# Odd chunks' feed-forward redistributed over the next batch's stages: 4, 4, 24 and 16 steps

## The chip, the cores and the metric

One core of one Trainium2 chip. The metric is the device time of one launch in microseconds (us). The engines are named as in the profile: PE is TensorE (PEld its weight loads), DVE is VectorE, ACT is ScalarE, POOL is GpSimd, SP is SyncE, which here issues all DMAs.

## The reference, cut to what matters

Two transformer layers on x (4 batches, 1024 tokens, 512 features) with a context of 64 tokens per batch. Cut to its shape:

```python
# layer 0: attention of x to the context, 16 heads, biased, then a layer norm
x = ln(softmax(q(x) @ k(ctx).T / 8 + 2 * fside) @ v(ctx) @ wo + bo + x)
# layer 1
x = attn(ln1(x), ln1(x)) + x        # self-attention, 16 heads of 32, 8-bit rounding of q, k, v, weights
x = attn(ln2(x), ctx) + x           # context attention, the same rounding
a, g = split(ln3(x) @ ff_w1 + ff_b1)   # 512 -> 2 x 2048
x = a * gelu(g) @ ff_w2 + ff_b2 + x    # 2048 -> 512
```

All unrounded products are made of three matmuls (high by high, high by low, low by high part), written by `three` (L1720).

## The kernel before, in words

A batch is two chunks of 512 tokens (CH), so there are eight chunks n = 0 to 7. For each batch the program runs four kinds of stage: `cross(n)` for both chunks (context attention of layer 0, the layer norms, and the projections q1, k1, v1), then for each chunk `self_attention(n)` and `middle(n)` (output projection, layer norm, second context attention, layer norm). I call them the A, S and M stages of a chunk. The feed-forward of a chunk has no stage of its own. Its 48 steps (F_STEPS, L45: four each of g0 a0 g1 d0 a1 g2 d1 a2 g3 d2 a3 d3) are hosted by later stages: each step is 12 matmuls of 128x512, in four quarters of three, into PSUM bank 6 or 7 in turn. A "g" step is taken out of PSUM by ACT (L1226), and the fourth is followed by a Gelu over all four (L1232); an "a" step is multiplied in by DVE (L1514), then split by ACT (L1218) and POOL (L1008); a "d" step is added to x by DVE (L1477). A step's bank must be emptied before the second step after it can begin (`wait_empty` in `feed`, L1899).

Every engine walks the same list of slots, and each slot of a stage may host quarters; `host_quarters` (L72) makes the list, `feed` on each engine takes from it what falls to that engine. Each engine executes strictly in this written order. A has 18 slots: slot 0, slots 1 to 11 beside the softmax steps, slots 12 to 15 before the transposes of the four 128-token tiles (`norm_T`, L1976 to L1978), called the tail here, and two more that PE fills with nothing. S has 71 slots, one per unit of 128 queries and one head. M has 23: 0 to 5 output projection, 6 to 9 projection q2, 10 to 18 the second context attention, 19 to 22 the last transposes.

Even chunks (FROM_S, L88) are hosted by the S and M stages of the next chunk, 28 and 20 steps. Odd chunks 1, 3 and 5 (`begins_in_A`, L93; FROM_A, L89) are hosted by both A stages, then S and M of the next batch's first chunk: 8, 8, 18 and 14 steps. So A, A, S, M of chunks 2, 3, 2, 2 host chunk 1; S and M of chunk 3 host chunk 2; and so on. Chunk 7's feed-forward runs alone at the end.

In M, PE's slot 12 hosts its quarters and then issues the third of the four score products s2 (L2066 to L2079), slot 13 the fourth and the first transposes of weights p2T, slot 14 the second p2T and the first weighted sum. DVE's slot s does the softmax parts in the order of L1649 to L1686: its hosted evictions of the slot before, then s2's maximum and subtraction, then the sum of the tile before, then w2T.

The feed-forward's weights come in 24 pieces (pairs of 512 KB, `load_piece` L660 on SP), two per letter of F_ORDER, into three slots, and a fourth (slot 3) for chunks that begin in A. Slot 3 lies over q1 and k1 of the odd chunk, slots 0 and 1 over the projection weights of the A stages; hence the first pieces of such a chunk use slots 3 and 2 in turn (L135), and two pieces wait for the end of A (L792 to L795). A piece is loaded when the last step of the piece that held its slot before has been filled (PIECE_LAST, PIECE_NEXT, L139 to L141); at such a step SP goes through the pieces v in rising order (L698 to L703). The pieces v = 22 and 23 both end with step 47 (PIECE_END, L50).

Of the kernel before, what the change touches and what calls it, by code (L numbers as in the profile page):

```python
# [19 lines left out]
NC = S // CH  # L20
# [51 lines left out]
def host_quarters(in_A, in_S, m_slots):  # L72

    ends = []
    for c in range(NC if in_A else 0):
        for s in range(A_SLOTS):
            ends.append(4 * in_A * c + (4 if s < A_TAIL else (12, 19, 26, 32)[min(s - A_TAIL, 3)]))
    first, start = 4 * NC * in_A, len(ends)
    for s in range(S_SLOTS):
        ends.append(min(first + 4 * in_S, first + 4 * in_S * (s + 1) // (S_SLOTS - 1)))  # L80
    for s in range(M_SLOTS):
        ends.append(first + 4 * in_S + 4 * sum(1 for m in m_slots if m <= s))
    assert ends[-1] == 4 * NF
    return Plan(ends, range(start, start + S_SLOTS))

FROM_S = host_quarters(0, 28, [s for s in range(M_SLOTS) if s not in (16, 21, 22)])  # L88
FROM_A = host_quarters(8, 18, (0, 1, 2, 3, 4, 6, 10, 11, 12, 13, 15, 17, 19, 21))  # L89
ALONE = Plan([4 * (k + 1) for k in range(NF)])  # L90


def begins_in_A(n):  # L93
    return n % NC == NC - 1 and n < CHUNKS - 1
# [34 lines left out]
def piece_order():  # L129

    slot, nth, last, count, latest = {}, {}, {}, [0] * 4, [None] * 4
    for n in range(CHUNKS):
        for v in range(PIECES):
            if begins_in_A(n):
                i = (3, 2)[v % 2] if v < 8 else (v - 8) % 3  # L135
            else:
                i = (v + 1) % 3
            count[i] += n > 0
            slot[n, v], nth[n, v], last[n, v] = i, count[i], latest[i]  # L139
            latest[i] = (n, v)  # L140
    return slot, nth, last, {key: after for after, key in last.items() if key is not None}  # L141
# [118 lines left out]
def build(nc, a, out):  # L260

    ctx = ExitStack()
    with ctx:
# [210 lines left out]
        def wait_filled(eng, key):  # L474

            i, n = FILL[key]
            eng.wait_ge(filled[i], n + 1)
# [75 lines left out]
        def _(sp):  # L553
# [139 lines left out]
            def feed(n, plan, i):  # L693

                if n == 0:
                    for v in pieces_due(plan, LAG_KEEP, i):
                        keep_piece(v)
                for k in steps_ending(plan, i):  # L698
                    for v in range(PIECES):
                        after = PIECE_NEXT.get((n, v))  # L700
                        if PIECE_END[v] == k and after is not None:
                            if not (begins_in_A(after[0]) and after[1] in (0, 8, 9)):
                                load_piece(*after)  # L703

            def load_x(n):
# [48 lines left out]
            def cross(n):  # L754

                b, c = divmod(n, NC)
                if n == 0:
                    load_x(0)
                    load_block((0, "M0"))
                    load_batch(0)  # L760
                    for i in range(3):
                        load_fbias(n, i)
                    load_block((0, "N0"))
                    load_block((0, "M1"))
                if c == 0:
                    load_x(n + 1)
                if n < NC:
                    load_prep(PREP_IN[n][0])
                for i in range(3, 7):
                    load_fbias(n, i)  # L770
                load_block((n, "N1"))
                load_fbias(n, 7)
                load_block((n, "q1"))
                load_block((n, "k1"))
                load_block((n, "v1"))
                if n == 0:
                    for key in FIRST:
                        keep_block(key)
                if n < NC:
                    keep_prep(PREP_IN[n][0])  # L780
                    if n == 1:
                        load_prep(PREP_IN[n][1])
                else:
                    for s in range(A_SLOTS):
                        feed(NC * b - 1, FROM_A, A_SLOTS * c + s)
                if c == 0:
                    for i in range(3):
                        load_fbias(n + 1, i)
                    load_block((n + 1, "M0"))
                    load_block((n + 1, "N0"))  # L790
                    load_block((n + 1, "M1"))
                elif n > NC:  # L792
                    wait_filled(sp, ("q1", n, 3))
                    for v in (8, 9):
                        load_piece(NC * b - 1, v)  # L795
                if n == 1:
                    keep_prep(PREP_IN[n][1])
                if c == NC - 1:
                    wait_block_used(sp, (n, "k1"))
                    sp.wait_ge(rounded.sem, rounded.at(("q1", n, 3)))  # L800
                    turn_queries(n - 1)
# [547 lines left out]
        def _(dve):  # L1349
# [172 lines left out]
            def cross(n):  # L1522
# [54 lines left out]
                host(A_TAIL + NT)  # L1577
                host(A_TAIL + NT + 1)
                if n % NC == NC - 1 and n > NC:
                    wait_filled(dve, ("f", NC * (n // NC) - 1, PIECE_END[6]))  # L1580
                for m in range(HG):
                    quantise(("q1", n, m), q1[n % NC][:, m, :])
                for m in range(HG):
# [563 lines left out]
```

## Time and profile before

| what | us |
|---|---|
| median of 3 runs | 3425.3 (3423.97 to 3429.12) |
| the profiled execution's own time | 3415.72 |
| its span (first to last instruction) | 3413.9 |
| PE busy in the span | 2951.5 (86%) |
| DVE busy | 2205.9 (65%) |
| ACT busy | 1671.2 (49%) |
| POOL busy | 1515.0 (44%) |

The time is about 1.8 us more than the span, for what lies around it. Busy time of PE is modelled and includes waiting in its pipeline. A row of a stretch gives its ends and length, then busy us and instructions (x) of PE, PEld, DVE, ACT and POOL (of PE and PEld alone where only they have some), PEclk, the DMA share and GB/s. A row of a timeline gives start, length, engine, line and operation. Where a row gives an idle time in brackets, the name behind the arrow is what ended it. PEclk is the granted TensorE clock, 1.00 for 2.4 GHz and 0.50 for 1.2 GHz.

### The profile page before, as it was taken

To read this page: it belongs to the slowest core of one execution; us is meant where nothing else is said; L and a number is where in the kernel's file an instruction comes from. 1 tells how busy PE (TensorE), PEld (TensorE's weight loads), DVE (VectorE), ACT (ScalarE), POOL (GpSimd) and SP (SyncE) were. 2 spreads that over 40 slices of the span, in tenths; PEclk is the share of its full clock that TensorE was granted. 3 is DMA by queue.
4 is the path that set the end of the run, shared out by engine and by line. 5 is a ranking of instruction groups with operands and counts; after the bars stand their busy time and mean duration, and the time that the engine had idled before them with its cause. 6 is when DMAs were issued, how large, how long until landed. Compare 5 with 4: busy or idle time off the path is not lost.

```text
span 3413.9 us, 50797 instructions
## 1 busy us (share of the span) xinstructions
PE 2951.5 (86%) x19712; PEld 2143.4 (63%) x19712; DVE 2205.9 (65%) x3543; ACT 1671.2 (49%) x2690; POOL 1515.0 (44%) x1182
## 2 busy tenths in 40 slices
PE   7677686887899899799889889899988989889999
PEld 6555445556677656566667656656777746656777
DVE  4456695883666596786565597687565588588521
ACT  5332572783333484574433375376333276387321
POOL 3554353663645253454455154354364154355321
PEclk9888657998999899899999999999999989999999
DMA  8653102334444213323453313313453322232444
GB/s 273 222 201 133 56 1 111 127 122 185 156 163 151 81 63 124 130 87 149 133 180 115 117 51 128 130 70 130 145 190 99 142 75 100 95 122 75 169 153 160
DMA packets 199758, 436.40 MB, mean 128 GB/s; under 512 B 94944, under 2 KB 103392, under 8 KB 182368
## 3 DMA queue, kind: packets, MB, share of 16 engines
q1 hardware_dynamic: 199520, 433.15, 35.6%
q8 instruction: 158, 2.59, 0.3%
q14 instruction: 80, 0.66, 0.1%
HBM read 363.38 MB, written 65.54 MB: 126 GB/s over the span
## 4 chain that ended last, share of the span: by engine, by line
PE 54%; DVE 24%; ACT 8%; issue 6%; POOL 4%; DMA 3%; SPq 1%; POOLq 0%; DVEq 0%; ACTq 0%
PE psum L1722 16%; PE psum L1724 14%; PE psum L1723 14%; DVE mx L1603 8%; DVE w1T L1622 4%; PE psum L2018 4%; ACT e L1293 2%; PE psum L2006 2%; DVE den L1609 2%; ACT psum L1180 2%; DVE gate L1514 1%; DMA unsplit<-in_L_xattn_ff_w 1%; ACT ht_hi L1179 1%; POOL w_lo L898 1%; PE psum L2032 1%
## 5 line engine op out<-in xcount | busy, mean ns | idle before, releaser
L989 POOL TENSOR_SCALAR w1b<-e,rec 128x1024 f16<-128x1024 f32 x512 | 574.5, 1122 | 696.3 <-DVE rec L1611 506.2
L1603 DVE TENSOR_REDUCE mx<-psum 128x1 f32<-128x1024 f32 x512 | 621.7, 1215 | 50.0 <-PE psum L2007 50.0
L1293 ACT ACTIVATE e<-psum,nb,scale 128x1024 f32<-128x1024 f32 x512 | 617.5, 1206 | 16.9
L1722 PE MATMUL psum<-h_hi,fw_hi 128*128 128x512 f32 x1024 | 463.3, 452 | 31.6 <-DVE h_lo L1379 10.0
L1723 PE MATMUL psum<-h_lo,fw_hi 128*128 128x512 f32 x1024 | 415.6, 406 | 0.0
L1724 PE MATMUL psum<-h_hi,fw_lo 128*128 128x512 f32 x1024 | 414.6, 405 | 0.0
L1622 DVE TENSOR_SCALAR w1T<-psum 128x1024 bf16<-128x1024 f16 x512 | 348.3, 680 | 92.0 <-PE psum L2018 87.2
L2018 PEld LDWEIGHTS psum<-ident,w1b 128*128 128x128 f16 x4096 | 259.8, 105 | 231.4 <-issue 192.4
L2018 PE MATMUL psum<-ident,w1b 128*128 128x128 f16 x4096 | 350.7, 234 | 61.9 <-DVE w1T L1622 58.7
L904 POOL TENSOR_TENSOR rstd<-ve,mhalf 128x1 f32<-128x1 f32 x128 | 86.9, 679 | 484.9 <-DVE ve L1485 484.9
L1477 DVE TENSOR_TENSOR x<-psum,x 128x512 f32<-128x512 f32 x224 | 152.2, 684 | 226.8 <-PE psum L1724 226.1
L1722 PEld LDWEIGHTS psum<-h_hi,fw_hi 128*128 128x128 f32 x1024 | 198.5, 194 | 152.3 <-issue 98.7
L1287 ACT ACTIVATE nb<-mx,nscale 128x1 f32<-128x1 f32 x512 | 149.8, 293 | 257.8 <-DVE mx L1603 249.1
L1722 PE MATMUL psum<-w_hi,ht_hi 128*128 128x512 f32 x640 | 257.9, 403 | 20.4 <-DVE e L1540 13.9
L1008 POOL TENSOR_TENSOR u_lo<-gate,u_hi 128x512 fp32r<-128x512 f32 x128 | 164.4, 1287 | 203.0 <-ACT u_hi L1218 197.3
L1723 PE MATMUL psum<-w_lo,ht_hi 128*128 128x512 f32 x640 | 251.7, 393 | 0.0
L1724 PE MATMUL psum<-w_hi,ht_lo 128*128 128x512 f32 x640 | 251.5, 393 | 0.0
L1722 PE MATMUL psum<-fw_hi,u_hi 128*128 128x512 f32 x512 | 226.3, 442 | 28.4 <-POOL u_lo L1008 13.7
L898 POOL TENSOR_TENSOR w_lo<-mixed,w_hi 128x512 fp32r<-128x512 f32 x140 | 190.2, 1382 | 130.8 <-ACT w_hi L1187 130.8
L1724 PEld LDWEIGHTS psum<-h_hi,fw_lo 128*128 128x128 f32 x1024 | 200.7, 196 | 46.9
L1125 ACT ACTIVATE qt<-psum,rounder,inv 128x512 f32<-128x512 f32 x128 | 99.9, 780 | 247.4 <-PE psum L1724 244.0
L2007 PE MATMUL psum<-k_odd,q_turned 32*128 32x512 bf16 x512 | 219.7, 430 | 0.0
(180 smaller groups left out, 6114.3 us busy)
## 6 DMA issues: line engine op xcount, KB each, us to landing
fw_hi<-pieces SPq DMA_DIRECT2D x168, 512.0 KB, 3.3
fw_lo<-pieces SPq DMA_DIRECT2D x168, 512.0 KB, 4.3
w_hi<-kept SPq DMA_DIRECT2D x45, 1024.0 KB, 4.9
w_lo<-kept SPq DMA_DIRECT2D x45, 1024.0 KB, 7.2
mixed<-mixed SPq DMA_DIRECT2D x32, 1024.0 KB, 5.1
fbias<-in_fside_Bx16xSxS SPq DMA_DIRECT2D x64, 256.0 KB, 3.0
unsplit<-in_L_xattn_ff_w SPq DMA_DIRECT2D x24, 512.0 KB, 5.1
pieces<-fw_hi SPq DMA_DIRECT2D x24, 512.0 KB, 2.6
```

Of the source, the lines that this page charges most:

```text
L898: pool.tensor_tensor(w_lo[s][:, k, :], w_mixed[s][:, k, :], w_hi[s][:, k, :].bitcast(F32), ALU.subtract).then_inc(block_lo_done.sem, 1)
L989: pool.tensor_scalar(w1b[u % NH][:], e1[u % NE][:], rec1[:, u % 8:u % 8 + 1], HALF, ALU.mult, ALU.add).then_inc(w1_ready.sem, 1)
L1008: pool.tensor_tensor(u_lo[:, m, :], gate[:, m, :], u_hi[:, m, :].bitcast(F32), ALU.subtract).then_inc(u_lo_done.sem, 1)
L1293: act.activation(e1[s % NE][:], psum[:, i:i + 2, :].rearrange("p i n -> p (i n)"), ACT.Exp, bias=nb1[:, s % 4:s % 4 + 1], scale=scale[:, 0:1],
L1477: return emptied_bank(dve.tensor_tensor(xt, bank(bank_of(key)), xt, ALU.add), key)
L1603: dve.tensor_reduce(mx1[:, s % 4:s % 4 + 1], psum[:, i:i + 2, :].rearrange("p i n -> p (i n)"), AX, ALU.max).then_inc(maxed1.sem, 1)
L1622: emptied_bank(dve.tensor_scalar(w1T[u % 8][:].rearrange("p k q -> p (k q)"), bank(bank_of(key)).bitcast(FP16), -HALF, W_HIGH, ALU.add, AL ...
L1722: pe.matmul(o, s_hi, m_hi, start=first, stop=False)
L1723: pe.matmul(o, s_hi, m_lo, start=False, stop=False)
L1724: return pe.matmul(o, s_lo, m_hi, start=False, stop=last)
L2007: ins = pe.matmul(bank(i + 1), q1_turned[turned, hg, t * P:t * P + P], k1[1][turned, hg, :], start=True, stop=True)
L2018: ins = pe.transpose(bank(bank_of(key)).bitcast(FP16)[:, k * P:k * P + P], w1b[u % NH][:, k * P:k * P + P], ident16[:])
```

## The change

It changes where the quarters of chunks 1, 3 and 5 are placed. Each A stage hosts 4 steps in place of 8: slot 0 still has one, and slots 12 to 15 have 12 quarters in place of 28. S hosts 24 in place of 18. M hosts 16 in place of 14: slot 8 gets one, and slot 12 gets a second one. The pieces' slots, the two pieces loaded late and DVE's one guard wait follow from the new number, IN_A = 4. Nothing of the arithmetic, and nothing in the plans of the other chunks, is changed.

```diff
--- before.py
+++ after.py
@@ -74,7 +74,7 @@
     ends = []
     for c in range(NC if in_A else 0):
         for s in range(A_SLOTS):
-            ends.append(4 * in_A * c + (4 if s < A_TAIL else (12, 19, 26, 32)[min(s - A_TAIL, 3)]))
+            ends.append(4 * in_A * c + (4 if s < A_TAIL else (7, 10, 13, 16)[min(s - A_TAIL, 3)]))
     first, start = 4 * NC * in_A, len(ends)
     for s in range(S_SLOTS):
         ends.append(min(first + 4 * in_S, first + 4 * in_S * (s + 1) // (S_SLOTS - 1)))
@@ -86,7 +86,8 @@
 
 
 FROM_S = host_quarters(0, 28, [s for s in range(M_SLOTS) if s not in (16, 21, 22)])
-FROM_A = host_quarters(8, 18, (0, 1, 2, 3, 4, 6, 10, 11, 12, 13, 15, 17, 19, 21))
+IN_A = 4
+FROM_A = host_quarters(IN_A, 24, (0, 1, 2, 3, 4, 6, 8, 10, 11, 12, 12, 13, 15, 17, 19, 21))
 ALONE = Plan([4 * (k + 1) for k in range(NF)])
 
 
@@ -132,7 +133,7 @@
     for n in range(CHUNKS):
         for v in range(PIECES):
             if begins_in_A(n):
-                i = (3, 2)[v % 2] if v < 8 else (v - 8) % 3
+                i = (3, 2)[v % 2] if v < IN_A else (v - IN_A) % 3
             else:
                 i = (v + 1) % 3
             count[i] += n > 0
@@ -699,7 +700,7 @@
                     for v in range(PIECES):
                         after = PIECE_NEXT.get((n, v))
                         if PIECE_END[v] == k and after is not None:
-                            if not (begins_in_A(after[0]) and after[1] in (0, 8, 9)):
+                            if not (begins_in_A(after[0]) and after[1] in (0, IN_A, IN_A + 1)):
                                 load_piece(*after)
 
             def load_x(n):
@@ -791,7 +792,7 @@
                     load_block((n + 1, "M1"))
                 elif n > NC:
                     wait_filled(sp, ("q1", n, 3))
-                    for v in (8, 9):
+                    for v in (IN_A, IN_A + 1):
                         load_piece(NC * b - 1, v)
                 if n == 1:
                     keep_prep(PREP_IN[n][1])
@@ -1577,7 +1578,7 @@
                 host(A_TAIL + NT)
                 host(A_TAIL + NT + 1)
                 if n % NC == NC - 1 and n > NC:
-                    wait_filled(dve, ("f", NC * (n // NC) - 1, PIECE_END[6]))
+                    wait_filled(dve, ("f", NC * (n // NC) - 1, PIECE_END[IN_A - 2]))
                 for m in range(HG):
                     quantise(("q1", n, m), q1[n % NC][:, m, :])
                 for m in range(HG):
```

## Rows read from the trace of the kernel before

**Rows 1.** The page: its first line, and the chain that ended last by engine.

```profile
span 3413.9 us, 50797 instructions
...
PE 54%; DVE 24%; ACT 8%; issue 6%; POOL 4%; DMA 3%; SPq 1%; POOLq 0%; DVEq 0%; ACTq 0%
```

**Rows 2.** Engines by stretch: A, S, M of chunk 4, then S, M of chunk 5.

```profile
1699.30:1823.20 123.90, 111.75 (x498) 88.83 (x497) 71.09 (x126) 45.79 (x63) 57.53 (x46) 0.97 0.46 161
...
1947.10:2102.20 155.10, 138.22 (x1369) 81.96 (x1369) 137.00 (x207) 117.32 (x216) 86.54 (x73) 0.92 0.18 68
2102.20:2197.80 95.60, 84.77 (x424) 67.22 (x424) 53.59 (x93) 27.82 (x37) 30.95 (x22) 0.95 0.32 116
2197.80:2377.10 179.30, 162.26 (x1490) 104.67 (x1489) 144.44 (x215) 133.18 (x235) 87.49 (x74) 0.94 0.29 107
2377.10:2484.30 107.20, 99.37 (x501) 78.63 (x498) 57.10 (x98) 32.81 (x43) 38.79 (x31) 1.00 0.47 171
```

**Rows 3.** PE's timeline in M of chunk 4: first matmuls of two groups of twelve.

```profile
2107.69 0.39 PE L1722 MATMUL psum<-h_hi,fw_hi 128*128 128x512 f32 x1
...
2110.41 0.39 PE L1722 MATMUL psum<-w_hi,ht_hi 128*128 128x512 f32 x1
```

**Rows 4.** DVE's timeline in the tail of A, chunk 4.

```profile
1757.37 0.68 DVE L1477 TENSOR_TENSOR x<-psum,x 128x512 f32<-128x512 f32 x1
...
1778.33 0.68 DVE L1477 TENSOR_TENSOR x<-psum,x 128x512 f32<-128x512 f32 x1
...
1784.37 1.50 DVE L1496 TENSOR_SCALAR z<-x,mv,rstd 128x512 f32<-128x512 f32 x1 [0.67 <-POOL rstd L904]
```

**Rows 5.** The same view in the tail of A, chunk 5.

```profile
1878.17 0.68 DVE L1477 TENSOR_TENSOR x<-psum,x 128x512 f32<-128x512 f32 x1
...
1907.10 0.55 DVE L1496 TENSOR_SCALAR z<-x,mv,rstd 128x512 f32<-128x512 f32 x1 [0.66 <-POOL rstd L904]
```

**Rows 6.** PE's timeline in the tail of A, chunk 0, which hosts nothing.

```profile
200.32 1.11 PE L1875 MATMUL psum<-ident,z 128*128 128x128 f32 x4 [4.19 <-DVE z L1496]
```

**Rows 7.** Stretches of S (chunks 4, 4, 5), instructions of L2006 alone, one per unit.

```profile
2019.00:2037.00 18.00, 2.75 (x6) 0.56 (x6) 0.81 0.16 61
2040.00:2092.00 52.00, 9.23 (x24) 2.17 (x24) 1.00 0.21 77
2292.00:2348.00 56.00, 9.23 (x24) 2.17 (x24) 1.00 0.26 95
```

**Rows 8.** ACT's timeline behind the Gelu in S of chunk 4: back to Exp.

```profile
2026.23 1.28 ACT L1293 ACT_TABLE_LOAD   x1
```

**Rows 9.** PE's timeline behind that Gelu.

```profile
2028.87 0.60 PE L2006 MATMUL psum<-k_even,q_even 32*128 32x512 bf16 x1 [3.58 <-ACT e L1293]
```

**Rows 10.** PE's timeline in the second context attention, M of chunk 4.

```profile
2155.01 0.50 PE L1722 MATMUL psum<-h_hi,fw_hi 128*128 128x512 f32 x1 [1.34 <-DVE gate L1514]
...
2157.86 0.61 PE L2078 MATMUL psum<-k,q2T 128*128 128x256 bf16 x4
...
2165.07 1.01 PE L2086 MATMUL psum<-ident,w2b 128*128 128x128 f16 x8 [6.15 <-DVE w2T L1672]
...
2169.22 0.76 PE L1722 MATMUL psum<-fw_hi,u_hi 128*128 128x512 f32 x1 [2.57 <-POOL u_lo L1008]
```

**Rows 11.** DVE's timeline in the same place.

```profile
2154.87 1.21 DVE L1656 TENSOR_REDUCE row_max<-psum 128x16 f32<-128x1024 f32 x1
...
2159.30 0.66 DVE L1514 SCALAR_TENSOR_TENSOR gate<-psum,col_L_xattn_ff_b,gate 128x512 f32<-128x512 f32 x1
2159.88 1.21 DVE L1656 TENSOR_REDUCE row_max<-psum 128x16 f32<-128x1024 f32 x1
```

**Rows 12.** Landing of the second piece's low part, issued at 2198.36 us, behind step 47.

```profile
DMA to landing us min/median/max: 7.7/7.7/7.7
```

**Rows 13.** PE's timeline at the start of S, chunk 5.

```profile
2199.95 0.47 PE L1722 MATMUL psum<-h_hi,fw_hi 128*128 128x512 f32 x1 [1.74 <-DVE h_lo L1379]
...
2206.67 0.38 PE L2006 MATMUL psum<-k_even,q_odd 32*128 32x512 bf16 x1 [1.91 <-ACT e L1293]
```

## The prediction

> **What bounds the kernel now.** I read the page first. PE is on 54% of the chain that ended last and DVE on 24% [rows 1], so a moved step is worth its PE time only in a stage where PE ends last. Next, the engines by stage [rows 2]. The stages of one batch repeat in the other two to within 0.3 us, so one batch is costed and taken three times. A of chunk 4 lasts 123.9 us (A of chunk 5 the same), S 155.1 with 18 hosted steps, M 95.6 with 14. In chunk 5, S lasts 179.3 with 28 and M 107.2 with 20. A step is twelve matmuls, 2.72 us on PE [rows 3]. Ten more steps are 27.2 us of matmuls, yet S grows by 24.2; six more in M are 16.3 us and M grows by 11.6. Neither stage takes steps for nothing, and a step taken out of A must give back about as much for the change to gain. So the timelines of three places decide: the tail of A, S, and the second context attention in M.
>
> **What the change does to A.** Four steps leave each A stage, all from slots 12 to 15. Were PE the bound there, each stage would give back 4 x 2.72 = 10.9 us. But the tail has a chain of its own on DVE: per token tile the residual, two variances, the norm, with POOL's rstd between. In chunk 0, which hosts nothing, PE waits 4.19 us for each z and takes 1.11 for its transposes: one tile per 5.30 us [rows 6]. In the loaded tail of chunk 4 the first residual starts at 1757.37, the last at 1778.33, the last z at 1784.37 [rows 4]. Bare, the last residual would start 3 x 5.30 = 15.9 us after the first, and its z 1784.37 - 1778.33 = 6.04 later: 21.9, against 27.0 now. That saves 5.1. The last z there takes 1.50 us, as POOL writes u_lo beside it, in chunk 5 only 0.55 [rows 4, 5]; the changed plan has only "g" steps in this tail, no u_lo, so 0.95 more, together 6.0. For the transposes that may run at 1.2 GHz again, as the 1.11 of chunk 0, I take 0.4 off: 5.6. In the tail of chunk 5 the first residual and the last z start 28.9 apart [rows 5]. There the changed plan has steps 5 and 6, two "a" evictions on DVE of about 0.7 before the last tile, so 21.9 + 1.4 = 23.3: 5.6 saved. Step 4, now in slot 0, is an "a" step, where step 8 was a "g" step: DVE, ACT and POOL each do a piece of it in the ramp of the softmax; I charge 1.1 (0 to 1.5). So 4.5. **A: -10.1 us per batch.** It is -21.8 if PE is the bound, and -8.5 if each tail keeps 0.8 more than counted. The Gelu behind step 3 moves behind h1T on ACT, ahead of the rounding of q1: its bank is wanted again by k1's third product, six products of 2.72 us later, and that covers it. The number of piece loads is unchanged; four fewer per A stage pass SP, and PE's waits for pieces in the tail go, which the DVE chain already contains.
>
> **S: 18 to 24 steps.** Outside the stalls, 24 units of chunk 4 take 52 us, 2.17 each, at 1.03 quarters per slot; in chunk 5 they take 56, 2.33 each, at 1.6 [rows 7]. Six more steps give 1.37 quarters per slot. From chunk 5 down along PE's price (0.23 quarters x 0.68 us) a unit is 2.18; on the straight line between the two it is 2.27. I take 2.23: 64 x 0.06 = 3.8 us, bounds 0.6 to 6.4. The twelve slots at the two ends (the first five, and 64 to 70, which have no product of their own) are PE's: 12 x 0.34 = 4 quarters more, at 0.68 us: + 2.7. Then a second Gelu. g1 now ends inside S, so ACT leaves Exp and comes back. ACT loads a table of 1.28 us on the way back [rows 8], and one as long on the way out. PE stands 3.58 us waiting for the exponential of a bank, and the matmuls behind run at half clock [rows 9]. The stretch around the Gelu took 18 us for 6 units [rows 7], where 6 x 2.17 = 13.0 would do: 5.0. **S: 3.8 + 2.7 + 5.0 = +11.5 us per batch,** bounds 8.3 and 14.5. The high bound is 0.6 x (24.2 - 2 x 5.0) + 5.0 = 13.5 and one for the start; the low bound comes down from chunk 5: four steps less and one Gelu less, 179.3 - 10.9 - 5.0 = 163.4.
>
> The Trainium skill's page "ScalarE: Activation LUTs", section "What ACT_TABLE_LOAD costs", speaks against the move: each change of table set costs a drain of some 1.38 us on top of the 1.28 us load. By that page the second Gelu would cost 2 x 1.38 us more wherever a drain is not yet in the 5.0, so +8 us over three batches, 3481 for the whole. The trace agrees on the 1.28 [rows 8] and shows no such drain as an instruction beside it, so I do not add it.
>
> **M: 14 to 16 steps.** The step in slot 8 falls into q2, which PE does without a pause: +2.7. The second step in slot 12 is the one meant for an idle place. That place exists: PE stands 6.15 us before the second p2T and 2.57 before the next step [rows 10]. But both lie behind slot 13, and slot 12 lies before s2's third product. I follow the program. Today step 43, in slot 13, waits 1.34 us for DVE's gate of step 41 and starts at 2155.01; the fourth s2 follows at 2157.86 [rows 10]. In the changed plan steps 41 and 42 stand in slot 12, so step 42 takes exactly that place: it waits for the gate of step 40, which DVE does at the same point. The third s2 follows only then, and DVE can begin its maximum at about 2158.4, where it began at 2154.87 [rows 11]. DVE does its hosted gates after two softmax parts, 4.43 us after that maximum starts (2159.30 - 2154.87). So the gate of 41 ends at 2158.4 + 4.43 + 0.66 = 2163.5. Only then can step 43 start, and it takes 2.85, 0.6 for s2: the fourth maximum starts at 2167.0, where it was 2159.88 [rows 11]. That is 7.1 us. The idle places behind keep their length, since DVE's order, not PE, sets them. If step 43 runs at half clock, having stood 5 us (behind 3.58 us matmuls did so [rows 9]), it is 2.4 longer. **M: 2.7 + 7.1 + half of 2.4 = +11.0 us per batch,** bounds 9.8 and 12.2 if this reading holds. The nearest slope, (107.2 - 95.6) / 6 = 1.93 a step, would give 3.9.
>
> **The next S.** The pieces of chunks 1, 3 and 5 now turn through the slots from v = 4 instead of 8, and 8 - 4 is no multiple of three. The last piece, 23, ends in slot 1 instead of 0. The next chunk's first piece is written for slot 1. Before, it followed piece 21 and was there early (step 43); now it can be loaded only behind step 47, and SP issues it second, after the piece that follows 22. Today's second load behind step 47 is issued at 2198.36 and lands 7.7 us later [rows 12], at 2206.0. PE's first hosted matmul of S, chunk 5, starts at 2199.95; it would wait until 2206.0 with every product queued behind it. The third unit waits anyway until 2206.67 for ACT [rows 13]; after the late piece PE has 0.9 of quarters, a product of 0.4 and 1.7 more before it, 2209.0 at full clock, 2211 at half. **+3.5 us,** bounds 2.3 and 6.1. Three such joints: chunks 2, 4 and 6.
>
> **Sum.** -10.1 + 11.5 + 11.0 + 3.5 = +15.9 us per batch, x 3 = +47.7. The profiled execution took 3415.7 us, giving 3463.4; it lies 9.6 below the median of the runs, 3425.3, and on that median the same sum gives 3473.
>
> **Rivals.**
> (a) *M takes its two steps on the slope of chunk 5.* Then -10.1 + 11.5 + 3.9 + 3.5 = 8.8, x 3 = 26.4: 3452. For it: in chunk 5 six more steps cost 11.6. Against it: none of those puts two steps ahead of one s2. Chance 0.18.
> (b) *The tail is PE's, and steps in M fill holes: faster.* Place: slots 12 to 15 of A. If PE, not DVE, ends last there, each A gives the full 10.9; if S comes at its low bound, and M pays only slot 8, then -21.8 + 8.3 + 2.7 + 2.3 = -8.5, x 3 = -25: 3400. It decides once the A stages give back over 17 us with M at 3.9. Against it: chunk 0's 5.30 us per tile, with no step at all [rows 6]. Chance 0.04.
> (c) *The late piece is hidden* by what ACT and DVE owe at the start of S anyway: 3473 - 10.5 = 3462.5. It is inside my own range; chance 0.13.
> That the plans do not do what they say I rule out by the sums: 4 + 4 + 24 + 16 = 48 steps, and the slots come out as named.
> My forecast has 0.63. Another 0.02 I leave to steps costing nothing in sum, no change.
>
> **Range and chances.** With every low bound, A at -12, and M at 3.9, the sum is 2.5 a batch, 3433; with every high bound -8.5 + 14.5 + 12.2 + 6.1 = 24.3, 3498. The ends together are unlikely: 3442 to 3492. A measurement of this kernel can tell about 0.2% (7 us) from no change. Faster 0.04, within 0.02, slower 0.94.
>
> **What would show it.** In the changed profile: tails of A about 5 us shorter, z and not matmuls ending PE's idle time; two Gelus in S of chunks 2, 4, 6, with 5 us around the new one; S near 166.6 and M near 106.6; in M an idle PE of about 5 us before step 43, ended by L1514; at the start of S of chunks 3, 5, 7 a wait for a piece until some 9 us after step 47, S near 182.8. I am wrong if A is shorter by over 8 us a stage, if slot 12's pair leaves the fourth s2 where it was, or if that first piece lands before h3T is split.

## The result, and the profile after

| | median us | range | runs |
|---|---|---|---|
| before, beside it | 3425.69 | 3423.97 to 3429.12 | 4 |
| changed | 3465.03 | 3463.63 to 3470.86 | 4 |

The two medians differ by 39.3 us; the ratio, taken over the runs and not from the two medians, is 1.0124 (95%: 1.0107 to 1.0141). I had forecast +47.7 and 3473, in a range from 3442 to 3492. The change is slower, as forecast. The profiled execution took 3465.73 us, in the middle of its runs, while the profiled one of before (3415.72) lies 9.6 us under its median. The two spans differ by 50.0 us, about 10 more than the medians, so sums of the two profiles come out that much high.

The page of the changed kernel: first line, engines, and the chain by engine [rows 1].

```profile
span 3463.9 us, 50791 instructions
...
PE 2961.9 (86%) x19712; PEld 2156.0 (62%) x19712; DVE 2205.8 (64%) x3543; ACT 1668.9 (48%) x2690; POOL 1511.8 (44%) x1182
...
PE 52%; DVE 25%; ACT 8%; issue 6%; POOL 5%; DMA 2%; SPq 1%; POOLq 0%; DVEq 0%; ACTq 0%
```

No engine has more to do. The busy times are those of before within 0.4%. On the chain PE's share fell by two points and DMA's by one, and those of DVE and POOL rose by one each. The page can't say where, so the stages must. Engines by stretch: A of chunk 4, A of chunk 5, S and M of chunk 4, S and M of chunk 5; they answer to [rows 2].

```profile
1715.90:1832.20 116.30, 101.41 (x451) 79.75 (x450) 66.23 (x122) 43.04 (x59) 52.36 (x42) 0.97 0.45 154
1832.20:1952.60 120.40, 101.87 (x451) 80.26 (x449) 72.19 (x130) 36.43 (x50) 51.72 (x44) 0.94 0.32 112
1952.60:2117.10 164.50, 150.87 (x1441) 94.83 (x1441) 140.75 (x211) 120.65 (x219) 83.81 (x71) 0.95 0.23 84
2117.10:2225.00 107.90, 92.99 (x454) 73.49 (x450) 53.52 (x94) 29.94 (x40) 33.53 (x24) 0.92 0.31 112
2225.00:2409.30 184.30, 162.96 (x1490) 105.39 (x1489) 144.46 (x215) 132.93 (x235) 87.18 (x74) 0.92 0.29 104
2409.30:2518.00 108.70, 100.91 (x501) 79.67 (x498) 57.16 (x98) 33.00 (x43) 38.74 (x31) 0.98 0.47 169
```

The means over the three batches, in us (the stages begin at the same instructions in both traces). Both kernels were profiled a second time, each in an execution of its own (the experiments "before again" and "the change again"); the fifth column is the difference between those two.

| stage | before | after | difference | difference of the repeats | forecast |
|---|---|---|---|---|---|
| A of chunks 2, 4, 6 | 124.0 | 116.7 | -7.3 | -5.6 | -5.6 |
| A of chunks 3, 5, 7 | 123.9 | 120.3 | -3.6 | -6.2 | -4.5 |
| S of chunks 2, 4, 6 | 155.1 | 163.4 | +8.2 | +9.7 | +11.5 |
| M of chunks 2, 4, 6 | 95.7 | 107.9 | +12.2 | +12.5 | +11.0 |
| S of chunks 3, 5, 7 | 179.3 | 184.2 | +4.9 | +1.4 | +3.5 |
| sum of one batch | | | +14.4 | +11.8 | +15.9 |

Three batches make +43 in the first pair of traces and +35 in the second. Their mean is the +39 of the medians. The remaining 7 us of the two spans lie in stages that the change doesn't touch: M of chunks 3 and 5 +1.5 each, S of chunk 1 +2.8, and the end behind chunk 7 +1.6. Why, the last section says.

Two timelines show the large terms at work. The first is PE's timeline in the tail of A, chunk 4, and answers to [rows 6] more than to the loaded tail of before.

```profile
1779.97 0.66 PE L1876 MATMUL psum<-ident,z 128*128 128x128 f32 x4 [1.14 <-DVE z L1497]
...
1785.27 0.66 PE L1876 MATMUL psum<-ident,z 128*128 128x128 f32 x4 [2.57 <-DVE z L1497]
```

These are the first and the second tile. They and the third (1790.57) follow 5.30 us apart, exactly chunk 0's pace with no step at all [rows 6]. The fourth comes 4.32 behind the third (1794.89), as no further tile stands between its operations on DVE. PE now waits there for the z of DVE, and three quarters per tile cost nothing.

The second is the chain that ended last, in the second context attention of M, chunk 4 (start, length, what). It answers to [rows 10, 11].

```profile
2169.16 1.22 DVE e L1660
...
2171.99 0.67 DVE gate L1515
2172.70 0.57 PE psum L1723
...
2177.30 0.47 PE psum L2079 x4
2177.79 1.24 DVE row_max L1657
...
2181.87 0.67 DVE gate L1515
2182.59 0.80 PE psum L1723
...
2187.48 0.47 PE psum L2079 x4
2187.97 1.24 DVE row_max L1657
```

This is the loop that the prediction worked out. The gate of step 40 (2171.99) lets step 42 start, and its twelve matmuls stand ahead of the third s2 (2177.30). DVE's maximum and subtraction come next, then the gate of step 41 (2181.87). Only then can step 43 start, and the fourth s2 stands behind it (2187.48). On this path PE and DVE take turns, and neither hides the other.

### The profile page after: what moved, and what is told of

Same layout as the page of the kernel before. It is cut to its first block, busy times and chain, and to the rows that moved or that the text cites. A ratio compares the mean times of both kernels' runs of the same rounds, so it can differ in the third digit from the quotient of the medians.

```text
span 3463.9 us, 50791 instructions
## 1 busy us (share of the span) xinstructions
PE 2961.9 (86%) x19712; PEld 2156.0 (62%) x19712; DVE 2205.8 (64%) x3543; ACT 1668.9 (48%) x2690; POOL 1511.8 (44%) x1182
## 4 chain that ended last, share of the span: by engine, by line
PE 52%; DVE 25%; ACT 8%; issue 6%; POOL 5%; DMA 2%; SPq 1%; POOLq 0%; DVEq 0%; ACTq 0%
PE psum L1723 15%; PE psum L1724 14%; PE psum L1725 14%; DVE mx L1604 8%; DVE w1T L1623 4%; PE psum L2019 4%; ACT e L1294 2%; PE psum L2007 2%; DVE den L1610 2%; DVE stats L1482 1%; POOL w_lo L899 1%; DVE x L1478 1%; ACT psum L1181 1%; DVE gate L1515 1%; PE psum L2033 1%
## 5 line engine op out<-in xcount | busy, mean ns | idle before, releaser
L1723 PE MATMUL psum<-fw_hi,u_hi 128*128 128x512 f32 x512 | 230.9, 451 | 21.2 <-POOL u_lo L1009 15.2
L1724 PEld LDWEIGHTS psum<-h_lo,fw_hi 128*128 128x128 f32 x1024 | 203.8, 199 | 28.0
```

The source lines that it names most:

```text
L1723: pe.matmul(o, s_hi, m_hi, start=first, stop=False)
L1724: pe.matmul(o, s_hi, m_lo, start=False, stop=False)
```

## The experiments

All medians come with the ratio to the kernel before, run on the same chip.

**Before again.** The same kernel, once, to see how far two executions differ by stage.

> The kernel before, once more, for a second profile. The profile of before that the prediction used lay 9.6 us under the median of its runs. If that is spread between executions, some stages that the change does not touch (S of chunk 1 was 184.5 us before and 187.3 after; M of chunks 3, 5 and 7 grew by 1.5) are longer here too, by 5 to 10 us in sum, and the changed stages (A 123.9, S of chunk 4 155.1, M of chunk 4 95.6) stay within 0.5 us. If the untouched stages come out as in the first profile (184.5, 107.2), their growth belongs to the change and needs a cause.

3430.22 us, span 3428.4, 14.5 us longer than the profiled execution of before. S of chunk 1 took 184.0 (before 184.5). The stages that the change does touch stayed within 0.5 us only in part: S of chunk 4 took 153.1 (before 155.1), A of chunks 5 and 7 126.7 and 127.3 (before 123.9), and S of chunks 3, 5 and 7 180.7 in the mean (before 179.3). M of chunk 5 took the other of two values:

```profile
2383.40:2492.10 108.70, 100.84 (x500) 79.69 (x497) 57.18 (x98) 32.82 (x43) 38.67 (x30) 0.98 0.47 169
```

So the +1.5 us in M of chunk 5 is no effect of the change: the kernel before shows the 108.7 too [rows 2]. A stage is known to some 2 us, at times 3, even from its three repeats.

**The turn of the pieces.** The first piece of the next chunk gets back the place that it can be loaded into early.

```diff
-                i = (3, 2)[v % 2] if v < IN_A else (v - IN_A) % 3
+                i = (3, 2)[v % 2] if v < IN_A else (v - IN_A + 2) % 3
...
-                            if not (begins_in_A(after[0]) and after[1] in (0, IN_A, IN_A + 1)):
+                            if not (begins_in_A(after[0]) and after[1] in (0, 5, 6)):
...
-                    for v in (IN_A, IN_A + 1):
+                    for v in (5, 6):
```

> The changed kernel with the pieces' turn through the slots shifted by two (pieces 4, 5, 6 in slots 2, 0, 1), so that the last pieces end in slots 1, 2, 0 as before and the next chunk's first piece is loaded at step 43 again. Theory (late first piece): the wait of 8.8 us for fw_lo at the start of S of chunks 3, 5, 7 goes, S there falls from 184.4 back to about 180 (first four units 17.0 us back to 13.8), 3.5 to 5 us each: 3465 to about 3452. Rival (the piece's lateness is covered by what ACT and DVE owe there, and S grew by spread): 3462 to 3465, S unchanged.

3444.67 us, ratio 1.0057 (1.0045 to 1.0070), faster than I expected. The start of S, chunk 5, on PE's timeline, first in the changed kernel, then in this one; it answers to [rows 13].

```profile
2234.18 0.77 PE L1723 MATMUL psum<-h_hi,fw_hi 128*128 128x512 f32 x1 [8.84 <-DMA fw_lo<-pieces]
```

```profile
2220.08 0.47 PE L1723 MATMUL psum<-h_hi,fw_hi 128*128 128x512 f32 x1 [1.74 <-DVE h_lo L1380]
...
2226.78 0.60 PE L2007 MATMUL psum<-k_even,q_odd 32*128 32x512 bf16 x1 [1.90 <-ACT e L1294]
```

The piece's low part was issued at 2225.5 and landed 8.6 us later (forecast 7.7 [rows 12]):

```profile
DMA to landing us min/median/max: 8.6/8.6/8.6
```

Without that wait S of chunks 3, 5 and 7 is back at 179.1 in the mean (181.1, 178.1, 178.2), from 184.2 in the first profile of the change and 182.1 in its second. That is 9 to 15 us over the three joints. The medians give 15 to 17: the change lies 39.3 and 36.9 us above the kernel before in its two sets of runs, this one 21.9. M stays at 108.0, so the turn and M are separate costs.

**The second step of slot 12 into slot 14.** Everything else as in the change.

```diff
-FROM_A = host_quarters(IN_A, 24, (0, 1, 2, 3, 4, 6, 8, 10, 11, 12, 12, 13, 15, 17, 19, 21))
+FROM_A = host_quarters(IN_A, 24, (0, 1, 2, 3, 4, 6, 8, 10, 11, 12, 13, 14, 15, 17, 19, 21))
```

> The changed kernel with the second step of M's slot 12 moved to slot 14, behind the fourth s2 and the first p2T. Theory (two steps ahead of the third s2 hold up DVE's softmax chain by 10 us): the fourth maximum starts about 13 us after the first again, not 23, and the step fills the idle place before the second p2T; but step 44 in slot 15 then waits longer for u_lo of step 43, whose gate DVE does a slot later, some 4 to 5 us. M of chunk 4 from 107.8 to about 102 (98 if that wait stays at 3), 4 to 9 us per batch: 3465 to between 3438 and 3453. Rival (a step costs its matmuls and a half-clock start wherever it stands in this section): M within 1 us of 107.8, 3465.

3447.18 us, ratio 1.0065 (1.0053 to 1.0078). M fell from 107.9 to 103.3. PE's timeline in the second context attention, chunk 4:

```profile
2165.31 0.50 PE L1723 MATMUL psum<-h_hi,fw_hi 128*128 128x512 f32 x1 [1.41 <-DVE gate L1515]
...
2175.37 0.61 PE L2087 MATMUL psum<-ident,w2b 128*128 128x128 f16 x8 [2.00 <-DVE w2T L1673]
...
2183.98 0.77 PE L1723 MATMUL psum<-fw_hi,u_hi 128*128 128x512 f32 x1 [7.46 <-POOL u_lo L1009]
```

The 4.84 us wait for a gate is gone and the step fills a place that was idle. But the first "d" step, still in slot 15, now comes too soon behind its "a" step: PE stands 7.46 us for POOL's u_lo, where it stood 2.57 before [rows 10] and 3.02 in the change. The move gave 4.6 us back. Whether it gives more with that step one slot later, the next kernel tells.

**Both mended, and slot 15 to 16.** Steps 4, 4, 24, 16 as in the change; the turn of the second kernel; M's slots 0, 1, 2, 3, 4, 6, 8, 10, 11, 12, 13, 14, 16, 17, 19, 21.

> The changed kernel with the pieces' turn mended, the second step of slot 12 moved to slot 14 and the step of slot 15 to slot 16, so that POOL has u_lo of step 43 ready before step 44 is reached. Theory (M's 12 us are 2.7 for slot 8 and the rest DVE's chain held up by slot 12's pair; the 7.5 us wait for u_lo in the slot-14 variant is due to step 44 standing one slot behind 43): M of chunk 4 from 103.2 to 98 to 100, 3 to 5 us per batch under the slot-14 variant; with the turn's 5 us per batch the kernel comes to 3418 to 3428, about even with before. Rival (wait and half-clock start only move to the next step): M stays at 103, 3430 to 3433.

3424.28 us over 11 runs, ratio 1.0001 (0.9991 to 1.0011). M takes 97.2 with 16 steps, 1.5 more than before with 14. The idle places of PE in M, chunk 4, now hold the steps:

```profile
2157.63 0.50 PE L1723 MATMUL psum<-h_hi,fw_hi 128*128 128x512 f32 x1 [1.41 <-DVE gate L1515]
...
2167.69 0.66 PE L2087 MATMUL psum<-ident,w2b 128*128 128x128 f16 x8 [2.04 <-DVE w2T L1673]
...
2171.36 1.01 PE L2087 MATMUL psum<-ident,w2b 128*128 128x128 f16 x8 [2.44 <-DVE w2T L1673]
```

So the slowdown is these two things: the turn of the pieces, and which slot each step of M goes to. The redistribution with 4 steps in each A is by itself worth nothing. By this kernel's own stages the two A give back 10.4 a batch, S takes 8.3, M 1.5 and the next S 1.3: +0.7.

**The pair alone.** The kernel before, with slot 10's step of M put into slot 12 beside the one there (slots 11, 12, 12, 13), nothing else.

> The kernel before with one thing changed: of M's 14 steps the one in slot 10 goes to slot 12 as the second step there (slots 11, 12, 12, 13 in place of 10 to 13). A, S, the counts, the Gelus and the pieces' turn are those of before. Theory (the pair holds the third and fourth s2 back behind DVE's gates): from the first s2 maximum to the fourth 22 to 23 us in place of 12.9, M of chunk 4 from 95.6 to 104 or 105, +8 to +10 us per batch, 3423 to about 3449. Rival (what M lost in the changed kernel came from its 16 steps and from the later Gelu, not from the order): M 95 to 97, 3423.

3438.68 us, ratio 1.0049 (1.0035 to 1.0064), +14.5 us between the medians; the stages of M say 7.1 more each (102.8), +21. I had expected 3449. The 7 us between the two figures I can't place: they are of the size by which two executions of one kernel differ. The first and the fourth maximum of s2 in M, chunk 4, on DVE's timeline:

```profile
2155.39 1.23 DVE L1657 TENSOR_REDUCE row_max<-psum 128x16 f32<-128x1024 f32 x1 [0.74 <-PE psum L2079]
...
2177.16 1.22 DVE L1657 TENSOR_REDUCE row_max<-psum 128x16 f32<-128x1024 f32 x1 [4.83 <-PE psum L2079]
```

They stand 21.8 us apart, against 12.9 before (the first at 2147.01, the fourth at 2159.88 [rows 11]) and 23.3 after. So the pair is a cost of its own, without the rest of the change. M grows by 1.8 less than the maxima move apart, mostly because PE's wait for w2T shrinks from 6.15 us [rows 10] to 4.45, the value of the changed kernel.

**Two steps in each A, 28 in S.** Tail quarters 5, 6, 7, 8; M as in the change.

> The changed kernel with 2 steps in each A stage and 28 in S, M as it is (16). Theory (the tail of A is DVE's chain of 5.30 us per tile): A of chunk 4 stays within 0.5 us of 116.3, since the steps taken out had no eviction on DVE; A of chunk 5 falls from 120.4 to about 117.5, as it loses two evictions and the u_lo beside z. Rival (PE's matmuls set the tail): both A stages fall by 2 x 2.72 = 5.4 us, to 111 and 115. S of chunk 4 takes 4 more steps with the same two Gelus: by PE's price 2.0 to 2.7 each, so 164.5 to about 173 to 175. In sum +5 to +7 us per batch by the theory, 3465 to about 3482; 3458 to 3465 by the rival.

3462.38 us, ratio 1.0112 (1.0097 to 1.0128). I had expected 3482. I had overlooked that 23 - 2 is a multiple of three: the last piece falls into slot 0 again and the joint costs nothing (S of chunks 3, 5, 7 at 178 to 180.5), some 15 us. Engines in A of chunks 4 and 5 and S of chunk 4:

```profile
1718.40:1837.20 118.80, 100.27 (x426) 78.49 (x425) 66.19 (x122) 38.71 (x55) 52.39 (x42) 0.89 0.39 133
1837.20:1953.70 116.50, 96.94 (x427) 76.03 (x425) 67.50 (x126) 36.88 (x49) 46.82 (x40) 0.91 0.33 117
1953.70:2125.30 171.60, 160.34 (x1489) 103.86 (x1490) 143.75 (x215) 124.44 (x224) 89.10 (x75) 0.95 0.25 92
```

The first A, with two steps, is no shorter than with four (118.1 in the mean against 116.7, where I had expected it within 0.5): its tail is at the bottom, and PE's transposes in it take 1.11 us in place of 0.66, at a granted clock of 0.89 over the stage against 0.97. The second A, now without an "a" step's u_lo beside its last z, gives back 3.7 (116.6 against 120.3). S pays 9.8 for its four more steps (173.2 against 163.4), and M 1.4 less (106.5). The sum is a loss: 9.8 + 1.4 - 3.7 - 1.4 = 6.1 a batch, which the mended joint (5.1) hides from the total.

**Six steps in each A.** Tail quarters 9, 14, 19, 24, 20 steps in S, M and its slots as in the mended version, the turn set for 6, and pieces 6 and 8 the ones loaded late. Two more kernels split the 36 hosted steps of S and M otherwise: 21 and 15 (slot 8 empty), 23 and 13 (slots 6, 8 and 10 empty).

```diff
-IN_A = 4
-FROM_A = host_quarters(IN_A, 24, (0, 1, 2, 3, 4, 6, 8, 10, 11, 12, 12, 13, 15, 17, 19, 21))
+IN_A = 6
+FROM_A = host_quarters(IN_A, 20, (0, 1, 2, 3, 4, 6, 8, 10, 11, 12, 13, 14, 16, 17, 19, 21))
...
-                i = (3, 2)[v % 2] if v < IN_A else (v - IN_A) % 3
+                i = (3, 2)[v % 2] if v < IN_A else (v - IN_A + 1) % 3
```

> 6 steps in each A stage, 20 in S, 16 in M with M and the turn as in f1. g1 is again finished in A, so S has one Gelu and two steps more than before. Theory (of S's growth of 9 us about 5 is the second Gelu): S of chunk 4 is 155.1 plus 2 x 0.7 to 1.8, 157 to 159; A of chunk 4 gives back part of its 7 us (two evictions of step 4, 5 and a Gelu in the tail of the first), about 118 to 120, A of chunk 5 about 120 to 122. Rival (a second Gelu costs nothing much, six steps cost their matmuls): S by 9.4 / 6 = 1.6 a step, 158.3, so that the same plan with 24 steps minus 4 x 1.6 agrees; then S does not tell them apart, and the units around the missing Gelu must: under the theory no group of four units in slots 12 to 20 takes 12.7 us. Time 3410 to 3422.

> 6 steps in each A stage, 21 in S, 15 in M (slot 8 without, slot 14 with a step, 16 in place of 15). Against f2 one step goes from M's slot 8, where PE has no idle time, to S, where DVE still hides part of it. Theory: M 2.7 us shorter, S 0.7 to 1.8 longer, 1 to 2 us per batch: 3 to 6 us faster than f2, and under before by 5 to 12 us. Rival (S is bound by PE at this density): no difference to f2.

> 6 steps in each A stage, 23 in S and 13 in M, so that S has nearly the density of the changed kernel (24) with one Gelu where that one has two. S of chunk 4 was 155.1 with 18 steps and one Gelu, 158.4 to 158.9 with 20 and one, 160.6 to 161.8 with 21 and one, 164.3 with 24 and two. Theory of the prediction (the second Gelu costs about 5 us): S of chunks 2, 4, 6 with 23 steps and one Gelu is 164.3 - 2.3 - 5 = 157 to 160. Rival (the Gelu costs under 2 us in sum, the rest is the steps' 1.5 to 2 us each): 162 to 164. The whole: 3398 to 3410.

3403.53 us (3397.41 to 3404.54), ratio 0.9935 (0.9922 to 0.9947); 3403.82, ratio 0.9939 (0.9925 to 0.9953); 3403.82, ratio 0.9941 (0.9927 to 0.9956). All three beat both kernels, and differ by nothing that can be told. The first is 7 us faster than I had expected. The second I had expected 3 to 6 us faster than the first, and it isn't: without slot 8's step M fell by 3.0 (97.7 to 94.7), but S took 2.1 for it (158.9 to 161.0). That is also the one place where the price of a step in slot 8, 2.7 in the prediction, can be read by itself. The first of them, A and S of chunk 4:

```profile
1690.60:1808.30 117.70, 106.31 (x475) 84.09 (x474) 68.45 (x124) 44.43 (x61) 55.20 (x44) 0.97 0.46 161
...
1928.30:2086.70 158.40, 141.01 (x1393) 85.63 (x1393) 140.16 (x211) 115.62 (x213) 85.06 (x72) 0.94 0.20 74
```

With six steps A takes 117.7 and 120.0, as with four: 2 x 2 steps a batch that cost nothing there. In its tail PE still waits a little for z, as its timeline shows:

```profile
1766.61 0.66 PE L1876 MATMUL psum<-ident,z 128*128 128x128 f32 x4 [1.19 <-DVE z L1497]
...
1770.93 0.66 PE L1876 MATMUL psum<-ident,z 128*128 128x128 f32 x4 [0.22 <-DVE z L1497]
```

The four waits are 0, 1.21, 1.19 and 0.22 us, so the place is nearly full. DVE's chain itself is as long with six steps as with four: from the first residual to the last z 21.7 us (1748.62 to 1770.33; in the change 1772.58 to 1794.29). Against before, the stages give A -10.2, S +3.8, M +2.0 a batch, -13 in all, and the spans of the two profiles -15.2; the medians give -20 (the ratio -22), since the profiled execution of before lies 10 under its median. The kernel with 23 steps in S bounds the second Gelu's price, as its S, steps 12 to 34, has only the Gelu of g2, and that of g3 falls into M. Its S takes 161.1, where the change's 24 steps and two Gelus took 163.4 and, in the repeat, 164.7: 2.3 to 3.6 us for one step and one Gelu. That S lies between what I had expected by the theory (157 to 160) and by the rival (162 to 164). The units around the new Gelu (in the next section) give 2.2 for the Gelu by itself, not 5.

**Eight steps in each A, as before, 17 in S, 15 in M.** One step from S into M's slot 14, slot 15's to 16.

> The plan of before with A untouched (8 and 8 steps), one step moved from S (17) into M's real idle place: M 15, slots 13, 14, 16 in place of 13, 15. Theory (M of chunk 4 stands idle 6.15 and 2.57 us behind slot 13): the step is done in that idle time, M stays within 1 us of 95.6, S falls by 0 to 1.5: 0 to 4 us faster than before. Rival (a step in M costs 1.9 us on the slope of chunk 5, or delays the second weighted sum): M 97.5 or more, even with before or slower by up to 5 us.

3425.3 us over 11 runs, ratio 1.0004 (0.9994 to 1.0014). M took its fifteenth step for nothing (95.2 in the mean, against 95.7), but S, with one fewer, did not get shorter (156.0, 157.3, 157.9 against 155.1), and the whole is no faster, where I had expected 0 to 4 us. At 17 steps against 18 S gives nothing back. So the gain of the six-step kernels is A's.

**The change again**, beside the last two.

> The changed kernel once more, beside the others on one chip, for a second profile: S of chunk 1, which nothing in the change touches, 184.0 to 184.5 or 187.3 (both have been seen); the wait for fw_lo at the start of S of chunks 3, 5, 7 again 8 to 9 us each; S there 183 to 185. Ratio to before 1.0107 to 1.0141. If it is nearer 1.010, the mended turn is worth about 15 us, as the stages say, and not the 23 that the two ratios gave.

3461.10 us, ratio 1.0109 (1.0093 to 1.0124), the same result as the first time within its interval. Its stages are not quite the same: A 118.3 and 119.8, S of chunks 2, 4, 6 164.7, M 107.9, S of chunks 3, 5, 7 182.1, under the 183 to 185 that I had expected, though the wait for fw_lo is there again (8.48 us in chunk 3, 7.84 in chunk 5).

## Why the prediction was right, and where it was off

Direction, range and mechanism held. The forecast of +47.7 was 8 us high against the medians (+39.3), and 5 high against the five stages of the first pair of traces (+43). That the whole is closer than its terms is luck: they were off by -0.8 (A), -3.3 (S), +1.2 (M) and +1.4 (the next S). Point by point:

**A: -10.1 forecast, -10.9 measured (-11.8 between the repeats).** The tail is DVE's, at 5.30 us a tile. From the first residual to the last z it takes 21.7 us in chunk 4, as the 21.9 that I had worked out. In the first A 1.7 us more came back than counted. About half of that is the granted clock: in chunks 4 and 6 the first matmuls of the stage's first hosted step take 0.63 us each before and 0.39 after, 1.1 to 1.2 us for the step. That is no effect of the change: in its repeat those of chunk 4 take 0.63 again, and the first A gives back 5.6, as forecast. In the second A 0.9 less came back. The last z took 1.48 us, as POOL wrote the u_lo of an "a" step beside it, where I had counted on 0.55, and DVE's gate waited 0.73 us for PE. DVE's timeline in the tail of A, chunk 5, against [rows 5]:

```profile
1904.92 0.75 DVE L1515 SCALAR_TENSOR_TENSOR gate<-psum,col_L_xattn_ff_b,gate 128x512 f32<-128x512 f32 x1 [0.73 <-PE psum L1725]
...
1911.63 1.48 DVE L1497 TENSOR_SCALAR z<-x,mv,rstd 128x512 f32<-128x512 f32 x1 [0.66 <-POOL rstd L905]
```

Rival (b), that the tail is PE's, fell: with 2, 4 and 6 steps the first A takes 118.1, 116.7 and 117.7, with 8 it takes 124.0. The last two of the eight cost 6.3, more than their 5.4 us of matmuls, and in the tail of before (chunk 4) PE waits for no z at the first two tiles, 1.74 us at the third and 0.50 at the fourth. The third:

```profile
1780.65 0.66 PE L1875 MATMUL psum<-ident,z 128*128 128x128 f32 x4 [1.74 <-DVE z L1496]
```

So the rival was true of most of the old tail and not of the new one. The prediction took the two ends of this curve and never asked for its kink. That is where the gain lay.

**S: +11.5 forecast, +8.2 measured (+9.7 between the repeats): each of its three terms was mis-sized.** Units of L2007 alone, in S of chunk 4: the first eight, eight around the new Gelu, 29 of the steady part, and eight around the other Gelu, g2's.

```profile
1952.50:1968.90 16.40, 3.51 (x8) 0.74 (x8) 0.79 0.47 186
1968.90:1993.20 24.30, 3.30 (x8) 0.73 (x8) 0.91 0.12 45
1996.00:2060.00 64.00, 11.15 (x29) 2.62 (x29) 1.00 0.23 84
2064.80:2087.30 22.50, 3.30 (x8) 0.73 (x8) 0.92 0.07 29
```

The same eight and eight units of L2006 in the kernel before:

```profile
1947.00:1964.90 17.90, 4.16 (x8) 0.76 (x8) 0.62 0.27 114
1964.90:1985.70 20.80, 3.29 (x8) 0.73 (x8) 0.92 0.14 52
```

The first eight again in before again, and the second eight in the kernel with 23 steps, which has no Gelu there:

```profile
1954.50:1970.90 16.40, 3.73 (x8) 0.75 (x8) 0.79 0.29 121
```

```profile
1950.70:1972.80 22.10, 3.08 (x8) 0.72 (x8) 0.92 0.26 96
```

*The ends, 2.7 forecast.* The first eight took 16.4 against 17.9, at 0.79 granted clock against 0.62. But the kernel before took 16.4 too in its second profile, so that is no gain of the change, and against it the first eight cost nothing more. At the other end the last seven took 16.1 against 15.7.

*The new Gelu, 5.0 forecast.* The eight units around it took 24.3 against 20.8. Of these 3.5 the Gelu has 2.2 (24.3 against 22.1 with 23 steps and no Gelu there); the rest comes with the denser quarters. The other Gelu costs its 4.8: 22.5 for eight units, where eight steady ones take 17.7. So 5.0 was right for a Gelu, and wrong for this place. The eight units have a stall of their own (4.9 us between two starts in the kernel before, where 2.1 is usual). That this is why the price is lower there is my reading; no run moved the one against the other.

*The steady part, 3.8 forecast.* The pace came as I had taken it, 29 units in 64 us, 2.21 each against 2.23. The pace of before was misread: [rows 7] count 24 starts in 52 us, 2.17 each, but the starts of eight units there stand 17.0 and 16.7 us apart, 2.11 each. So the growth was larger: units 16 to 31 took 36.6 us in place of 32.7, and units 32 to 55, with one Gelu in either kernel, 2.2 more. That is 6.1, and from the first unit to the last -1.5 + 3.5 + 6.1 + 0.4 = 8.5 in chunk 4.

ACT's timeline around the new Gelu:

```profile
1985.00 1.28 ACT L1233 ACT_TABLE_LOAD   x1
1986.30 1.91 ACT L1233 ACTIVATE gate<-gate 128x2048 f32<-128x2048 f32 x1
...
1988.41 1.28 ACT L1294 ACT_TABLE_LOAD   x1
1989.71 1.20 ACT L1294 ACTIVATE e<-psum,nb,scale 128x1024 f32<-128x1024 f32 x1
```

Each operation starts 0.02 us or less behind its load, and the second load 0.02 behind the operation ahead of it. The drain of 1.38 us that the Trainium skill's page "ScalarE: Activation LUTs" gives in "What ACT_TABLE_LOAD costs" is not to be seen, and leaving it out was right. By an estimate from that page the whole would have been 3481, further off. The number of loads is also no higher than before (58 in either trace): the second Gelu of S is the one that the second A no longer has.

**M: +11.0 forecast, +12.2 measured.** The 2.7 for slot 8 is borne out by the two kernels with six steps in A, of which the one without that step had an M shorter by 3.0. The fourth maximum came 23.3 us behind the first, against 12.9: 10.4 more, where I had 7.1 and half of 2.4, 8.3. The missing 2.1 is clock: step 42 took 4.60 us and step 43 4.89, both of them at a low clock, against 2.85, and I had counted half a slow step (1.2) in all. In the run with the pair alone step 42 was at full clock, and the maxima moved 8.9 apart in place of 10.4. The idle place behind then shrank (w2T 6.15 to 4.45), which I had said would keep its length, and u_lo's wait grew by 0.45: 2.7 + 10.4 - 1.7 + 0.45 = 11.9. Rival (a), the slope of chunk 5, fell with this. I did "follow the program" here, and it paid: the pair's price was worked out from an instruction order and two rows, and the run with the pair alone shows it as +7.1 a stage.

**The next S: +3.5 forecast, +4.9 measured (+1.4 between the repeats).** The piece landed 8.6 us behind its issue, not 7.7, and PE's first step then ran its first matmul at half clock (0.77 us against 0.47). Taking the wait away gave back 5.1, or 3.0 from the change's second profile. The size of this term is thus known to 2 us only, and the forecast lies inside. Rival (c), that it is hidden, fell, by the medians too (15 to 17 us over three joints).

**The remainder.** Medians give +39.3, the profiles +50.0. I had compared the sum with one execution, and said that it lies 9.6 under the median; the same was not true of the changed kernel's profiled one. The spans of the second pair of profiles differ by 31.1. The mean of the two pairs is +40.6, and that of their five stages +39. So the profiles and the medians agree once each kernel is profiled twice; one pair of profiles alone was 8 to 11 us off.

What stays open: whether S of chunks 2, 4 and 6 needs its 155 us at the least. It took 153 to 158 with 17 and 18 steps alike, and no run here hosted fewer than 17.

## What to carry to other kernels

Before work is moved out of a stage, find the number at which that stage stops being the busy engine's, and move only that far: here two steps of the four that were moved out of each A bought nothing, and S and M paid for them. A profile of one execution does not find that number alone when its stages differ by 2 us between executions: compare medians, or profile both kernels twice. A piece of work put "into an idle place" must stand behind the wait that makes the place and ahead of nothing that feeds the other engine; here a second step in slot 12 costs 7 us a stage, and a step in slot 14 nothing. And whatever is numbered by such a plan, here a ring of buffers turned by v modulo three, must be looked at anew for its last member, as the joint to the next round is where its phase shows.

## What the runs showed of the hardware

**Stages have two lengths, whatever the kernel.** S of chunk 1, which no variant changes, took 184.0 to 184.5 us in nine traces and 187.2 to 187.3 in four (the changed kernel, its repeat, and those with 4, 4, 24, 16 mended and with 8, 8, 17, 15). Two traces, of the first kernel run again and of the changed one:

```profile
602.60:786.60 184.00, 162.96 (x1490) 104.61 (x1489) 151.82 (x215) 142.87 (x247) 118.61 (x86) 0.94 0.33 116
```

```profile
600.60:787.90 187.30, 165.27 (x1490) 106.19 (x1489) 151.36 (x215) 142.81 (x247) 118.53 (x86) 0.93 0.32 114
```

The M stages of chunks 3 and 5 take 107.2 or 108.7, in kernels of either kind. The same instructions are in both, and PE is busy longer at a lower granted clock. So a single stage in a single trace carries 1.5 to 3 us that no edit made.

**How long PE stood does not alone say whether the next matmuls run slow.** Behind 1.85 us of idle time in M of the changed kernel, step 42 was granted 0.63 of full clock, though the ten us before were at 1.00 with PE busy for 8.85 of them. Behind 2.08 us, in the kernel with the pair alone, the same step was at 1.00. The two steps by window, first the changed kernel (with the stretch before it), then that kernel:

```profile
2172.70:2177.30 4.60, 4.60 (x14) 3.50 (x15) 0.00 (x0) 0.63 (x1) 3.77 (x3) 0.63 0.97 288
...
2162.00:2172.00 10.00, 8.85 (x42) 6.47 (x40) 7.76 (x11) 3.89 (x4) 0.00 (x0) 1.00 0.60 212
```

```profile
2163.40:2167.00 3.60, 3.50 (x16) 2.47 (x16) 0.07 (x1) 0.63 (x1) 3.32 (x3) 1.00 1.01 308
```

After 4.8 us both ran slow. What decides between the two is not shown by any run here. For a step of twelve matmuls the slower clock costs 1.7 us (4.60 against 2.85 at full clock).
